# 24 tiles of 126 pixels that turn around the middle pixel, instead of 25 squares of 121, in a depthwise convolution on TensorE

## What is computed

```python
k = jnp.transpose(kernel, (1, 2, 0))[:, :, None, :]
y = lax.conv_general_dilated(x, k, window_strides=(1, 1), padding='SAME',
        dimension_numbers=('NHWC', 'HWIO', 'NHWC'), feature_group_count=ch)
return x + y
```

## Time and profile before

| | us |
|---|---|
| median of 3 runs (826.73 to 827.2) | 827.06 |
| the profiled execution | 826.83 |
| its span, first to last instruction | 825.0 |

### The profile page before, as it was taken

The page is one execution under the profiler, slowest core; times in us unless marked ns, Lnnn a source line. Parts: engine busy times, 40 slices in busy tenths (PEclk is TensorE's granted clock), DMA queues, the critical chain, the costliest instruction groups (busy, mean ns, idle before and its releaser), DMA issues.

```text
span 825.0 us, 20812 instructions
## 1 busy us (share of the span) xinstructions
PE 814.7 (99%) x7200; PEld 814.5 (99%) x7200; DVE 670.8 (81%) x2118; ACT 619.6 (75%) x1538; POOL 591.9 (72%) x389
## 2 busy tenths in 40 slices
PE   6999999999999999999999999999999999999998
PEld 6999999999999999999999999999999999999998
DVE  6888888878788887878888888878888887888886
ACT  5777777777777777777777777777777777777775
POOL 6768577696775867858668677685775867758662
PEclk9999999999999999999999999999999999999999
DMA  9999999999999999999999999999999999999975
GB/s 364 414 388 402 354 395 375 376 381 367 402 371 376 384 371 395 376 368 400 355 382 398 368 400 363 373 397 356 401 372 378 353 404 384 377 365 405 363 317 227
DMA packets 28759, 309.29 MB, mean 375 GB/s; under 512 B 3184, under 2 KB 3312, under 8 KB 4208
## 3 DMA queue, kind: packets, MB, share of 16 engines
q1 hardware_dynamic: 28656, 307.98, 97.1%
HBM read 158.55 MB, written 149.42 MB: 373 GB/s over the span
## 4 chain that ended last, share of the span: by engine, by line
PE 99%; POOL 0%; DMA 0%; issue 0%; ACT 0%; DVE 0%; DVEq 0%
PE sums L419 66%; PE sums L415 33%; POOL matrix L237 0%; DMA first<-consts 0%; POOL expanded L228 0%; POOL taps L219 0%; POOL spare L216 0%; POOL taps L214 0%; ACT y_out L307 0%; DVE y_out L357 0%; DVEq L95 0%
## 5 line engine op out<-in xcount | busy, mean ns | idle before, releaser
L419 PE MATMUL sums<-matrix,x_high 121*128 121x240 f32 (+3 forms) x4800 | 814.2, 278 | 0.0
L419 PEld LDWEIGHTS sums<-matrix,x_high 121*128 121x128 f32 x4800 | 730.7, 192 | 0.0
L415 PE MATMUL sums<-matrix,x_low 121*128 121x240 f32 (+3 forms) x2400 | 665.8, 277 | 6.8 <-POOL matrix L237 6.8
L307 ACT ACTIVATE y_out<-sums 128x220 f32<-128x220 f32 (+6 forms) x1248 | 420.5, 376 | 194.3 <-PE sums L419 175.8
L357 DVE TENSOR_TENSOR y_out<-sums,y_out 128x60 f32<-128x60 f32 (+5 forms) x1824 | 358.8, 227 | 144.6 <-ACT y_out L307 62.6
L415 PEld LDWEIGHTS sums<-matrix,x_low 121*128 121x128 f32 x2400 | 460.4, 192 | 6.9 <-POOL matrix L237 6.8
L265 POOL TENSOR_TENSOR x_low<-x_in,x_high 121x640 fp32r<-121x640 f32 x190 | 320.7, 1710 | 119.0 <-DVE x_high L331 119.0
L340 DVE TENSOR_TENSOR x_low<-x_in,x_high 121x1280 fp32r<-121x1280 f32 (+1 forms) x194 | 290.2, 1497 | 2.2 <-ACT x_high L297 2.1
L297 ACT ACTIVATE x_high<-x_in 121x640 fp32r<-121x640 f32 (+1 forms) x288 | 263.6, 916 | 7.3 <-DMA x_in<-x 7.3
L253 POOL TENSOR_TENSOR matrix<-expanded,mask 121x600 fp32r<-121x600 f32 x95 | 157.9, 1662 | 92.4 <-PE sums L419 90.5
L331 DVE CAST x_high<-x_in 121x640 fp32r<-121x640 f32 x96 | 68.1, 710 | 3.8 <-DMA x_in<-x 3.3
(11 more groups left out here) (5 smaller groups left out, 0.6 us busy)
## 6 DMA issues: line engine op xcount, KB each, us to landing
x_in<-x SPq DMA_DIRECT2D x95, 1600.0 KB, 10.2
y<-y_out SPq DMA_DIRECT2D x95, 1520.0 KB, 13.2
rest<-later SPq DMA_DIRECT2D x1, 1150.0 KB, 12.1
x_in<-x SPq DMA_DIRECT2D x3, 320.0 KB, 3.6
y<-y_out SPq DMA_DIRECT2D x1, 852.5 KB, 3.6
x_in<-x SPq DMA_DIRECT2D x1, 640.0 KB, 6.1
y<-y_out SPq DMA_DIRECT2D x1, 365.0 KB, 2.3
y<-y_out SPq DMA_DIRECT2D x1, 302.5 KB, 2.7
```

The lines of the kernel that those rows point to most:

```text
L307: act.activation(outputs(c, rows, cols), sums(c, t, rows, cols), ACT.Copy).then_inc(copied, 1)
L415: pe.matmul(target, x_low[c % SLOTS][0:PIXELS, at:at + IMAGES], window(c, strip, k, slice(HIGH, HIGH + 1)).squeeze(1), start=k == tile["sq ...
L419: product = pe.matmul(target, x_high[c % SLOTS][0:PIXELS, at:at + IMAGES], window(c, strip, k, slice(part, part + 1)).squeeze(1), start=Fa ...
```

## The change

The plane is cut another way. Four quarters of 6 tiles turn around the middle pixel (27, 27): a "flat" tile is 9 rows x 14 columns, a "tall" one 14 x 9, 126 pixels each; 24 x 126 = 3024, and the middle pixel is a 127th row of tile 5. A quarter has three banks of two tiles, 12 banks per channel. There are two matrices now, one for flat tiles (15 x 20 cells) and one for tall ones (20 x 15, stored with a pitch of 16). The masks that make them come by a transfer at the start. All four high parts are ACT's and all four low parts DVE's, in pieces of 768 columns (a quarter); POOL only makes matrices. The rows of `x` in memory are 3072 columns read out of a pitch of 3104.

```diff
+QUARTERS = (
+    (FLAT, (0, 14), (0, 9, 18)),
+    (TALL, (0, 14), (28, 37, 46)),
+    (FLAT, (27, 41), (28, 37, 46)),
+    (TALL, (27, 41), (0, 9, 18)),
+)
+SHAPES = ((15, 20), (20, 15))
+HIGH_AFTER = (1, 3, 5, 7)
+LOW_AFTER = (4, 6, 8, 10)
...
-                sp.dma_start(x_in[c % X_SLOTS][:, :], x[c, :, :]).then_inc(x_loaded[c % X_SLOTS], 16)
+                sp.dma_start(x_in[c % X_SLOTS][:, :], x[c, :, 0:IN_COLS]).then_inc(x_loaded[c % X_SLOTS], 16)
...
+                if piece == 0:
+                    sp.dma_start(mask[:, :, :], masks[:, :, :]).then_inc(masks_loaded, 16)
...
-            for a, b in LAST_STORES:
+            for t, done, end in ((TOP_BANKS, 0, split), (BANK_COUNT, split, OUT_COLS)):
+                sp.wait_ge(added, ADDS * c + ADDS_BEFORE[t])
...
+            def spread_taps(c):
+                if c:
+                    pool.wait_ge(matrix_step, 2 * KINDS * c)
+                for kind in range(KINDS):
...
+                    pool.tensor_copy(
+                        spread[kind][0:whole, :, :].rearrange("p h (d a e) -> p (h d) a e", d=TAPS, e=TAPS),
+                        rows.unsqueeze(2).broadcast_to(shape)).then_inc(spread_step, 1)
...
             def make_matrix(c):
+                pool.wait_ge(spread_step, KINDS * (c + 1))
...
+                    pool.wait_ge(sums_done, BANK_COUNT * (c - SLOTS + 1))
+                for kind in range(KINDS):
+                    shape = [whole, ROWS[kind] // TAPS, TAPS, COLS[kind]]
+                    for part in (HIGH, LOW):
+                        pool.tensor_tensor(
...
-                for piece in range(HEADS):
-                    split_low(c, piece)
...
             for c in range(CHANNELS):
+                for t in range(BANK_COUNT):
+                    copy_bank(c, t)
+                    if c + 1 < CHANNELS and t in HIGH_AFTER:
+                        split_high(c + 1, HIGH_AFTER.index(t))
...
             for c in range(CHANNELS):
+                for t in range(BANK_COUNT):
+                    add_seams(c, t)
+                    if c + 1 < CHANNELS:
+                        if t in LOW_AFTER:
+                            split_low(c + 1, LOW_AFTER.index(t))
...
             for c in range(CHANNELS):
+                for t, bank in enumerate(PLAN):
+                    kind, quarter = bank["kind"], bank["quarter"]
+                    if t % (BANK_COUNT // PIECES) == 0:
+                        if quarter < KINDS:
+                            pe.wait_ge(matrix_step, 2 * KINDS * c + 2 * (kind + 1))
+                        pe.wait_ge(low_ready, PIECES * c + quarter + 1)
                     wait_bank(c, t)
...
+                        pe.matmul(target, low, turned[HIGH], start=tile is bank["tiles"][0], stop=False,
+                                  skip_group_check=True)
+                        pe.matmul(target, high, turned[LOW], start=False, stop=False, skip_group_check=True)
+                        product = pe.matmul(target, high, turned[HIGH], start=False, stop=last, skip_group_check=True)
```

More of the change, by code:

```diff
@@ L65, in tiles_of_plane @@
[L65 to L78, removed]
@@ L81, with reach @@
[L81 to L94, removed]
+TURNED = KINDS * FILTER
+HIGH_AFTER = (1, 3, 5, 7)
+LOW_AFTER = (4, 6, 8, 10)
+CONSTS = GROUP * TURNED + TURNED
+LATER = (GROUPS - 1) * GROUP * TURNED
+def reach(at, size):
+    return max(0, at - HALO), min(SIDE, at + size + HALO)
@@ new lines, in banks_of_plane @@
+def banks_of_plane():
+    banks = []
+    for quarter, (kind, along, across) in enumerate(QUARTERS):
+        for n, v in enumerate(across):
+            deep = SHORT + (quarter == 0 and n == len(across) - 1)
+            short, long = reach(v, deep), (reach(along[0], LONG)[0], reach(along[-1], LONG)[1])
+            rows, cols = (short, long) if kind == FLAT else (long, short)
+            tiles = []
+            for k, u in enumerate(along):
+                a, b = reach(u, LONG)
+                y, x = ((*short,), (a, b)) if kind == FLAT else ((a, b), (*short,))
+                first_y, first_x = (v, u) if kind == FLAT else (u, v)
+                width = (x[1] - x[0] + 1) // 2 * 2
+                tiles.append(dict(
+                    at=(quarter * PER_QUARTER + n * PER_BANK + k) * IMAGES,
+                    pixels=PIXELS + (quarter * PER_QUARTER + n * PER_BANK + k == CENTRE_TILE),
+                    rows=(y[0] - rows[0], y[1] - rows[0]), cols=(x[0] - cols[0], x[0] - cols[0] + width),
+                    from_row=y[0] - (first_y - HALO), from_col=x[0] - (first_x - HALO)))
+            banks.append(dict(quarter=quarter, kind=kind, rows=rows, cols=cols, tiles=tiles,
+                              pitch=(cols[1] - cols[0] + 1) // 2 * 2))
+    return banks
@@ new lines, in rectangles, with plan_of_sums @@
+def rectangles(cells):
+    found, left = [], cells.copy()
+    while left.any():
+        y, x = np.argwhere(left)[0]
+        right = x
+        while right < SIDE and left[y, right]:
+            right += 1
+        bottom = y
+        while bottom < SIDE and left[bottom, x:right].all():
+            bottom += 1
+        left[y:bottom, x:right] = False
+        found.append(((int(y), int(bottom)), (int(x), int(right))))
+    return found
+def plan_of_sums(banks):
+    covered = np.zeros((SIDE, SIDE), bool)
+    earlier = []
+    for bank in banks:
+        cells = np.zeros((SIDE, SIDE), bool)
+        cells[slice(*bank["rows"]), slice(*bank["cols"])] = True
+        (bank["copy"],) = rectangles(cells & ~covered)
+        seams = sorted(rectangles(cells & covered), key=lambda r: (r[0][0] < r[0][1] and (
+            [n for n, e in enumerate(earlier) if meet(e, r)] or [-1])[-1]))
+        bank["adds"] = []
+        for seam in seams:
+            after = [n + 1 for n, e in enumerate(earlier) if meet(e, seam)]
+            bank["adds"].append((seam, after[-1] if after else 0))
+            earlier.append(seam)
+        covered |= cells
+    return len(earlier)
@@ L95, in build, with meet @@
+def meet(a, b):
+    return all(p[0] < q[1] and q[0] < p[1] for p, q in zip(a, b))
+PLAN = banks_of_plane()
+ADDS = plan_of_sums(PLAN)
+BANK_COUNT = len(PLAN)
+ADDS_BEFORE = [sum(len(b["adds"]) for b in PLAN[:n]) for n in range(BANK_COUNT + 1)]
+TOP_BANKS, TOP_ROWS = 6, min(b["rows"][0] for b in PLAN[6:])
+def build(nc, consts, masks, later, x, out):
     with ExitStack() as ctx:
@@ L111, in build @@
-        expanded = sbuf("expanded", [P, GROUP, 2, EXPANDED], F32)
-        mask = sbuf("mask", [P, MATRIX], F32)
+        taps = sbuf("taps", [P, GROUP, KINDS, 2, FILTER], F32R)
+        spare = sbuf("spare", [P, GROUP, KINDS, FILTER], F32)
+        spread = [sbuf(f"spread{k}", [P, 2, TAPS * COLS[k]], F32) for k in range(KINDS)]
         warm = sbuf("warm", [P, 1], F32)
         psum = ctx.enter_context(nc.psum_tensor("sums", [P, BANKS, BANK], F32))
-        at = GROUP * FILTER
-        centre = first[0:PIXELS, at:at + FILTER]
@@ L118, in build @@
[L118 to L123, removed]
+        whole = PIXELS + 1
+        centre = first[0:whole, GROUP * TURNED:CONSTS].rearrange("p (k f) -> p k f", f=FILTER)
@@ L136, in bank_of @@
-        def bank_of(c, t):
-            return (c * TILE_COUNT + t) % BANKS
-        def sums(c, t, rows, cols):
[L141 to L145, removed]
+            return slice(piece * PIECE_COLS, (piece + 1) * PIECE_COLS)
@@ L147, in outputs, with plane_of @@
+        def plane_of(c, t):
+            bank = PLAN[t]
+            height = bank["rows"][1] - bank["rows"][0]
+            return psum[:, (c * BANK_COUNT + t) % BANKS, 0:height * bank["pitch"]].rearrange(
+                "p (h w) -> p h w", w=bank["pitch"])
+        def sums(c, t, rows, cols):
+            top, left = PLAN[t]["rows"][0], PLAN[t]["cols"][0]
+            return plane_of(c, t)[:, rows[0] - top:rows[1] - top, cols[0] - left:cols[1] - left]
         def outputs(c, rows, cols):
@@ L205, in split_taps @@
                         pool.wait_ge(later_loaded, 16)
[L206 to L214, removed]
+                    pool.wait_ge(spread_step, KINDS * GROUP * group)
@@ new lines, in corners_of_tiles @@
+def corners_of_tiles():
+    for kind, along, across in QUARTERS:
+        for v in across:
+            for u in along:
+                yield (kind, v, u) if kind == FLAT else (kind, u, v)
+def lay_out_input(x):
+    plane = x.transpose(3, 1, 2, 0)
+    rows = np.zeros((CHANNELS, P, IN_PITCH), x.dtype)
+    for n, (kind, top, left) in enumerate(corners_of_tiles()):
+        high, wide = (SHORT, LONG) if kind == FLAT else (LONG, SHORT)
+        rows[:, :PIXELS, n * IMAGES:(n + 1) * IMAGES] = plane[:, top:top + high, left:left + wide].reshape(
+            CHANNELS, PIXELS, IMAGES)
+        if n == CENTRE_TILE:
+            rows[:, PIXELS, n * IMAGES:(n + 1) * IMAGES] = plane[:, CENTRE, CENTRE]
```

313 lines of the change are left out of this document (104 added, 209 removed).

## The result

The changed kernel takes 841.31 us (median of 4 runs, 841.07 to 841.76), beside 827.13 us of the kernel before, run with it: 1.0172 times as long, 95% interval 1.0155 to 1.019. It is slower by 1.7%; the forecast was 796.3 us. The profiled execution took 841.13 us with a span of 839.3.

What follows compares the result with a forecast made beforehand. The prediction took PE to be the bound, paced by pairs of load and matmul at 112.7 ns each. Its terms: 826.83 - 32.5 + 0.9 + 1.1 = 796.3 us, range 789 to 815 us.

Steps and rivals of the forecast that it cites:

- the pace: On PE, each pair of load and matmul takes 112.7 ns whatever the columns; new period 8.11 us per channel.
- The removal of 288 matmuls: On PE, 6912 matmuls instead of 7200, at 112.7 ns each: -32.5 us.
- The start: Before PE's first matmul, larger splits and one more copy, mask transfer hidden: +0.9 us, bounds +0.5 to +1.3.
- The end: After the last matmul, a larger last store (+0.9) and three seams instead of two (+0.2): +1.1 us.
- ACT: ACT's copies and four high parts take 7.2 us of each channel's 8.11; cost nothing.
- POOL: POOL's products, copies and splits take 4.8 us per channel, bounds 4.0 to 5.7; hidden.
- DVE: DVE's seams, low parts and cast take 7.4 us of each channel's 8.11, bounds 7.0 and 9.1; cost nothing.
- Transfers: DMA: as a term, 386 GB/s, cost nothing; as a rival, transfers bind and give 814 us, 6 in 100.
- The shared port: DVE's low parts and POOL's instructions hold each other up, DVE paces the kernel: 887 us, 12 in 100.
- Columns as the pace: On PE, the columns streamed set the matmul time: 810 us, 8 in 100.
- The sign I had named for it: On PE, tiles with 252 columns run at a pace well over that of tiles with 176.
- late low parts: A low part coming too late stalls PE at a channel's start, losing as much as gained; 3 in 100.

Runs made afterwards that it cites:

- experiment 1: The kernel before with both matrices begun 8 bytes later in SBUF, nothing else: 894.36 us, 1.0814 times the kernel before.
- the dense version: The changed kernel with matrices stored at a pitch of 18 (flat) and 14 (tall) instead of 20 and 16: 799.09 us, 0.9661 times the kernel before.
- experiment 2: The changed kernel, from channel 4 on streaming one probe-tensor window per two channels, by a table of windows: 288 columns take 133 or 173 ns per matmul.

## Why the prediction was wrong

**The step that failed** is the pace: "So I take the pace to be that of the pairs of load and matmul, whatever the columns", and with it that up to 252 columns "at that even pace should not show". The two windows compared in the earlier trace rows were of 240 and 182 columns, and both lay under the floor of some 112 ns: 240 columns are 15 rows of 16 from column 0, 15 x 4 = 60 groups; 182 are 13 rows of 14 from column 1, 13 x 4 = 52. From two points under a floor I concluded that there is only the floor. The changed kernel lies above it in most of its tiles: 18 x 14 columns are 72 groups and take 130 to 133 ns, 16 x 14 are 64 and 117 ns, 18 x 12 from column 2 are 72 and 139 ns (means of a tile's three matmuls; the first of these three, which follows a tile under the floor, takes 153, the last 130); 18 x 12 from column 0, with 54, takes 115. The mean is 119.3 ns instead of 112.7, and (8.587 - 8.11) x 96 = 46 us is the miss but for 1 us. Added up over the 24 windows of a channel, the rule as the expectation of experiment 1 states it (111.7 ns, or the groups x 1.667 ns + 10.5 ns) gives 8.585 us where 8.587 was measured, and for the dense version 8.134 where 8.147 was measured.

The trace of before had the sign, and I did not read it. In its groups by shape 208 columns have a longer mean than 240:

```profile
L419 PE MATMUL sums<-matrix,x_high 121*128 121x240 f32 x1728 | 308.3, 277 | 0.0
...
L419 PE MATMUL sums<-matrix,x_high 121*128 121x208 f32 x1152 | 206.3, 280 | 0.0
```

Some of the 13 x 16 windows begin in column 1 and touch 5 groups in each of 13 rows, 65, just over the floor. The means are of modelled durations, but the starts agree: these windows take 118 to 119 ns, the 13 x 16 from column 0 only 110 to 114. A smaller operand that takes longer spoke against "whatever the columns" before the change was made.

**The removal of 288 matmuls** was right as a mechanism. In the dense version PE's busy time is 784.3 us, 30.4 less than before, against the forecast of 32.5; what is left goes with a mean of 113.1 instead of 112.7 ns, with windows of 63 groups at 116 to 123 ns. Its time, 799.1 us, is 2.8 over my 796.3; but the forecast was made for the layout that takes 841, so this doesn't bear it out.

**The start** was +1.4 instead of +0.9 us. The chain (start us, us) answers to the earlier trace rows:

```profile
1.65 4.02 DMA mask<-masks
5.80 2.42 POOL matrix L266 x2
8.27 0.51 PE sums L368
```

The mask, which I had called hidden, lands at 5.67, and POOL waited 0.3 us for it; the two products took 1.21 us each instead of 1.03; and the first split began at 2.92 instead of 2.67. The splits added their 0.6 us, and the second copy next to nothing. **The end** was +1.3 instead of +1.1.

**ACT** was forecast at 7.2 us per channel and has 685.1 / 96 = 7.14; the sum is right because two errors cancel, high parts of 835 ns (forecast 890) and neighbours that overlap by 57 ns (forecast 70). **POOL** was forecast at 4.8 and has 5.2, inside its bounds. **DVE** was forecast at 7.4 and has 633.8 / 96 = 6.6: the seams came as said (259 ns, forecast 257), the low parts at 1.01 us instead of 1.17, even below my lower bound of 1.06. (The slack of 7% to 14% in the port's rival was 9% to 14% by my own sums.) **Transfers** cost nothing, as said: ACT's high parts wait 7.0 us for `x`, ACT's copies twice, 3.5 us in all, for a store of `y` before 47 us, and PE for neither; the dense version moves 381 GB/s in its shorter period.

**The rivals.** The shared port did not decide. The low parts as one tile's view has them (ns minimum / median / maximum):

```profile
L314 DVE TENSOR_TENSOR x_low<-x_in,x_high x384: 945/948/1593, 5.8 to 826.0; 128x768 fp32r<-128x768 f32 x192
```

Half of them take at most 948 ns, 3 ns over the fastest. By the start times in the trace, 55 of the 384 take over 1.1 us, 1.38 on average, and each of these began while a POOL product or split was running; 67 others, in which POOL's began second, take no longer than 960 ns. So a low part pays only where POOL was first, and that was one in seven and not two of four as my sum had it. The rule of the Trainium skill (SBUF — State Buffer, Who interferes with whom), an exclusive lock for whichever began first, fits both. Columns as the pace was nearer in kind, but wrong as well: it gave 810 us, and 216 columns at 115 or at 139 ns can't come from it. The sign I had named for it, "a pace of tiles with 252 columns well over that of tiles with 176", did appear, and would have been put down to columns without experiments 1 and 2. Transfers and late low parts did not hold PE up: it has no idle time after its first matmul.

None of the rivals had slower matmuls as the bound on the slow side, so the 12 in 100 for slower were right in sign by luck: their mechanism, the port, cost PE nothing.

## What to carry to other kernels

Before taking a pace as independent of the operand's size, compare all shapes in the trace by their means, and look for one that breaks the order. For moving operands of this rounded float32 type count the aligned groups of 16 bytes that the rows of the window touch, not the columns: above the floor a first column off the multiple of 4, or a width that spills into one more group, costs as much as four more columns in every row. Check it in the trace, since one window here (14 columns from column 3) did not follow. Where windows have the full width of the matrix, storing it without gaps makes them one run. A narrower window can lose by it (18 x 12 from column 0 went from 115 to 119 ns); here the dense layout as a whole was worth 42 us of 841 and turned a loss of 1.7% into a gain of 3.4%.

## What was not expected of the hardware

- The moving operand of this rounded float32 type is paid by aligned groups of 4 floats: 1.667 ns per group at a granted clock of 1.00, plus 10 to 20 ns (tiles of the changed kernel and the table of experiment 2), above a floor of some 112 ns for a load and a matmul. An offset of 8 bytes cost 67 us in the old kernel.
- Open: why 14 columns from column 3 cost as 4 groups per row (173 ns) and not as 5; why the constant is some ns larger for some windows (16 wide from column 0: 180 ns, where 12 wide from column 1, also 96 groups, takes 173); and what sets the floor, which was not tried alone.
